# Attention blocks ordered by halves of the queries, with two buffers for the normalised block

## What is computed

```python
# layer 0: 16 heads of 32, rotary, biases, key mask
h = ada_norm(x, cond, ln1...)                   # norm, then scale and shift
q, k, v = heads(h @ wq + bq), heads(h @ wk + bk), heads(h @ wv + bv)
q, k = rotary(q), rotary(k)
attn = softmax(where(mask, q @ k.T / sqrt(32), -inf))
x = x + merge(attn @ v) @ wo + bo
x = x + gelu(ada_norm(x, cond, ln2...) @ ff_w1 + ff_b1) @ ff_w2 + ff_b2
# layer 1: 16 query heads on 4 key and value heads, no rotary
sh1, sc1, g1, sh2, sc2, g2 = split(silu(cond) @ wc.T + bc, 6)
x = x + g1 * (gqa(norm(x) * (1 + sc1) + sh1) @ wo.T)
x = x + g2 * (gelu((norm(x) * (1 + sc2) + sh2) @ w1.T + b1) @ w2.T + b2)
```

## Time and profile before

| what | us |
|---|---|
| median of 3 runs | 4369.27 (4364.93 to 4376.75) |
| the profiled execution, own time | 4378.7 |
| its span, from the first to the last instruction | 4376.9 |
| TensorE busy | 3913.1 |
| VectorE busy | 2427.8 |
| GpSimd busy | 1636.8 |
| ScalarE busy | 1618.2 |
| first score matmul starts | 136.80 |

### The profile page before, as it was taken

How to read it: one execution, slowest core, us unless ns; L and a number is a source line. 1 busy time by engine, 2 the same in 40 slices (tenths; PEclk the granted TensorE clock), 3 DMA queues, 4 the chain that set the end, 5 groups by cost and what they waited for, 6 DMA issues and landing times.

```text
span 4376.9 us, 53519 instructions
## 1 busy us (share of the span) xinstructions
PE 3913.1 (89%) x20400; PEld 1527.1 (35%) x20400; DVE 2427.8 (55%) x3944; ACT 1618.2 (37%) x2807; POOL 1636.8 (37%) x907
## 2 busy tenths in 40 slices
PE   6978899898998989989899998998899898989999
PEld 4312343233432234322243223432244223432234
DVE  3756635655455644556454666366554665556652
ACT  1456313553125531255411553135521553125521
POOL 2367212573115732156410563026510563115620
PEclk9889999989999999999999999999899999999999
DMA  4232242221422123232122021311122112310112
GB/s 133 59 90 107 69 106 73 68 62 56 102 74 64 54 78 91 76 80 67 67 87 87 15 65 57 105 37 42 37 87 92 28 35 71 100 57 18 62 55 95
DMA packets 140701, 307.44 MB, mean 70 GB/s; under 512 B 20336, under 2 KB 60292, under 8 KB 139552
## 3 DMA queue, kind: packets, MB, share of 16 engines
q10 hardware_dynamic: 50944, 174.62, 12.5%
q1 hardware_dynamic: 89504, 129.40, 11.3%
HBM read 225.56 MB, written 36.72 MB: 60 GB/s over the span
## 4 chain that ended last, share of the span: by engine, by line
PE 67%; DVE 13%; DMA 8%; POOL 5%; issue 4%; ACT 2%; SPq 1%; ACTq 0%; POOLq 0%; DVEq 0%
PE ps L774 11%; PE ps L775 11%; PE ps L776 11%; PE ps L954 8%; PE ps L875 7%; PE ps L937 6%; PE ps L811 6%; DMA dcopy<-inverses 5%; DVE mcol L1434 5%; PE ps L969 3%; POOL sums L691 3%; PE ps L828 2%; DMA inverses<-inverse 2%; ACT probs L1116 1%; DVE turn L1356 1%
## 5 line engine op out<-in xcount | busy, mean ns | idle before, releaser
L691 POOL TENSOR_TENSOR sums<-probs 128x1024 f32<-128x1024 f32 x480 | 1141.9, 2392 | 1513.4 <-ACT probs L1116 998.3
L1434 DVE TENSOR_REDUCE mcol<-ps 128x1 f32<-128x512 f32 x2048 | 1284.8, 684 | 543.1 <-PE ps L875 541.3
L1116 ACT ACTIVATE probs<-ps 128x512 f32<-128x512 f32 x2048 | 1105.0, 604 | 905.2 <-PE ps L937 614.4
L937 PE MATMUL ps<-qs,ks 98*128 98x512 f16 x2048 | 800.1, 402 | 190.0 <-ACT probs L1116 188.0
L875 PE MATMUL ps<-ks,qs 97*128 97x512 f16 x2048 | 809.7, 401 | 104.3 <-DVE mcol L1434 72.2
L954 PE MATMUL ps<-probs,v_sb 128*32 128x512 f32 x4096 | 597.2, 659 | 0.0
L1262 ACT ACTIVATE sums<-ps,cols 128x512 f32<-128x512 f32 x256 | 175.8, 687 | 1127.2 <-PE ps L776 1127.2
L875 PEld LDWEIGHTS ps<-ks,qs 97*128 97x128 f16 x2048 | 205.2, 100 | 723.3 <-DVE mcol L1434 385.9
L1520 DVE CAST probs<-sums 128x512 f16<-128x512 f32 x256 | 123.7, 483 | 501.8 <-ACT sums L1262 501.3
L774 PE MATMUL ps<-aT,ring 128*128 128x512 f16 x1024 | 392.2, 383 | 0.0
L775 PE MATMUL ps<-aT,ring 128*128 128x512 f16 x1024 | 391.2, 382 | 0.0
(11 more groups left out here) (106 smaller groups left out, 3221.9 us busy)
## 6 DMA issues: line engine op xcount, KB each, us to landing
ring<-halves ACTq DMA_DIRECT2D x208, 512.0 KB, 3.4
qs<-hl SPq DMA_DIRECT2D x192, 128.0 KB, 4.0
ring<-halves SPq DMA_DIRECT2D x48, 512.0 KB, 6.1
ring<-in_weights ACTq DMA_DIRECT2D x39, 512.0 KB, 4.4
halves<-ring ACTq DMA_DIRECT2D x37, 512.0 KB, 2.9
dcopy<-inverses SPq DMA_DIRECT2D x64, 256.0 KB
ks<-hl SPq DMA_DIRECT2D x120, 128.0 KB, 4.3
probs<-in_x SPq DMA_DIRECT2D x8, 1024.0 KB, 6.7
```

What stands on the lines that cost most here:

```text
L691: pool.tensor_tensor(sums[:, m % SUM_SLOTS, :, :], prob(u - 2), prob(u), ALU.add).then_inc(sum_set[0].sem, 1)
L937: pe.matmul(ps[:, bank, :], ks[0:K_EXP, key_set(i, hh), key_head(i, hh, h), P * kt:P * kt + P], qs[0:K_EXP, qc, h, :], start=True, stop=Tr ...
L1116: act.activation(prob(u)[:, e, :], ps[:, w % SCORE_BANKS, :], ACT.Exp).then_inc(exp_done.sem, 1)
L1434: dve.tensor_reduce(mcol[:, blk % 2, 4 * j + qt, half:half + 1], src, AX.X, ALU.max).then_inc(n_free[0], 1)
```

## The change

- `block_of` puts the halves of the queries outermost: blocks 0 to 3 are all heads of queries 0 to 511. The query stack `qs` is indexed by the half of the heads and overwritten by the second half of the queries at the steps 20 and 32. In layer 0 the second half of the keys is now used from block 2 on (before: block 4), so its projections, rotations and transfers move forward (`TURNS` in place of `ROTATE_AT`), and the maxima of block 2 start at step 8 (`MAX_AT_K`).
- `out_tile` waits for four finished blocks; its steps are 54 to 57 (n = 2 and 3 for the second half), `ln2` at 61 and 62, `norm_apply` of the second half at n = 4.
- `ocopy` has two buffers. `normalise` stands after addition 6 of the next block, ScalarE's `finish` at `w` = 11 of the block after that, GpSimd's after addition 1 there.
- Block 7 does not go through DRAM: VectorE inverts the whole `dcopy` (`invert_last`).
- `load_again` moves from `u` = 68 to 98, the bias additions of layer 0 to the additions 50 to 58, `deviation` of `ln2` from addition 56 to 55.
- At the start GpSimd's wait for the rows (`s_rows`) moves behind the first norms and builds.

```diff
--- before.py
+++ after.py
@@ -26,22 +26,23 @@
-O_AT, D_AT, HI_AT, INVERT_AT = 7, 12, 27, 4
+O_AT, D_AT, HI_AT, INVERT_AT, NORM_AT, LO_AT = 7, 12, 11, 4, 6, 1
...
-MAX_AT_0 = (0, 2, 5, 7, 9, 11, 14, 16, 18, 20, 23, 25, 27, 29, 32)
-WO_AT = 55
-LN2_AT = 62
-BIAS_AT = (40, 41, 42, 43, 48, 49, 54, 55)
-ROTATE_AT = ((1, 2, 6), (5, 6, 16), (14, 15, 31), (26, 28, 59))
+MAX_AT_K = (0, 2, 5, 7, 9, 11, 14, 16, 18, 20, 23, 25, 27, 29, 32)
+WO_AT = 54
+LN2_AT = 61
+BIAS_AT = (50, 51, 52, 53, 54, 55, 56, 58)
+TURNS = ((("k", 1, 0), -1, 1, 5), (("k", 1, 1), 3, 4, 11), (("q", 0, 1), 11, 13, 29), (("q", 1, 1), 25, 27, 57))
...
 def layer(i):
@@ -49,17 +50,18 @@
 def block_of(blk):
-    hh, r = divmod(blk, 4)
-    return hh, r // 2, r % 2
...
-def max_step(u):
+    qc, r = divmod(blk, 4)
+    return r // 2, qc, r % 2
...
+def max_step(i, u):
...
-        at = MAX_AT_0 if blk + 1 == 4 else MAX_AT
+        at = MAX_AT_K if layer(i) == 0 and blk == 1 else MAX_AT
...
-        items = [] if blk + 2 == 4 else [(blk + 2, k) for k in range(2 * (s - 14), 2 * (s - 13))]
+        items = [] if layer(i) == 0 and blk == 0 else [(blk + 2, k) for k in range(2 * (s - 14), 2 * (s - 13))]
@@ -85,12 +87,12 @@
-        for step, key in ((1, ("k", i, 1, 0, 0)), (2, ("k", i, 1, 0, 1)), (3, ("v", i, 1, 0)), (4, ("v", i, 1, 1)),
-                          (5, ("k", i, 1, 1, 0)), (6, ("k", i, 1, 1, 1)), (8, ("v", i, 1, 2)), (9, ("v", i, 1, 3))):
+        for step, key in ((0, ("k", i, 1, 0, 0)), (1, ("k", i, 1, 0, 1)), (2, ("v", i, 1, 0)), (3, ("k", i, 1, 1, 0)),
+                          (4, ("k", i, 1, 1, 1)), (6, ("v", i, 1, 1)), (7, ("v", i, 1, 2)), (9, ("v", i, 1, 3))):
...
-    for qc in range(2):
+    for hh in range(2):
...
-            at[11 + part if qc == 0 and layer(i) == 0 else 13 + 12 * qc + part] = [("q", i, 1, qc, part)]
+            at[11 + part if hh == 0 and layer(i) == 0 else 13 + 12 * hh + part] = [("q", i, hh, 1, part)]
@@ -119,8 +121,8 @@
-        if n in (3, 4):
-            keys += [("wo", i, 2 * n - 2), ("wo", i, 2 * n - 1)]
+        if n in (2, 3):
+            keys += [("wo", i, 2 * n), ("wo", i, 2 * n + 1)]
@@ -142,12 +144,13 @@
 def first_fills(j):
...
-        keys = [(kind, j, 0, th, part) for kind in "kq" for th in range(2) for part in range(2)]
+        keys = [("k", j, 0, th, part) for th in range(2) for part in range(2)]
+        keys += [("q", j, hh, 0, part) for hh in range(2) for part in range(2)]
...
-        keys += [("q", j, 0, th, part) for th in range(2) for part in range(2)]
+        keys += [("q", j, hh, 0, part) for hh in range(2) for part in range(2)]
@@ -277,7 +280,7 @@
-        ocopy = sb("ocopy", [P, D], F32)
+        ocopy = sb("ocopy", [P, 2, D], F32)
@@ -369,7 +372,8 @@
-        inv_part = count("inv_part", 8)
+        inv_part = count("inv_part", 7)
+        inv_last = count("inv_last", 1)
@@ -510,13 +514,13 @@
-                            dst = qs[r0:r0 + rows, th, heads, :]
+                            dst = qs[r0:r0 + rows, hh, heads, :]
...
             def put_rows(i, blk):
...
-                d = qs[97:98, qc, 4 * g:4 * g + 4, :]
+                d = qs[97:98, hh, 4 * g:4 * g + 4, :]
@@ -557,12 +561,12 @@
-                        if s == 9:
+                        if s == 7:
...
-                            put_stack(("q", i, 1, s // 32, part))
+                            put_stack(("q", i, s // 32, 1, part))
@@ -591,9 +595,6 @@
-                totals_out(i, 7)
-                inverse_in(i, 7)
-                if j < NB:
@@ -711,49 +712,57 @@
             def normalise(i, blk):
...
-                pool.wait_ge(inv_set.sem, inv_set.at(i, blk + 1))
-                pool.tensor_tensor(ocopy[:, :], ocopy[:, :], dcopy[:, :], ALU.mult).then_inc(a_set.sem, 1)
+                if blk < 7:
+                    pool.wait_ge(inv_set.sem, inv_set.at(i, blk + 1))
+                else:
+                    pool.wait_ge(inv_last.sem, inv_last.at(i, 1))
+                pool.tensor_tensor(ocopy[:, blk % 2, :], ocopy[:, blk % 2, :], dcopy[:, :], ALU.mult).then_inc(a_set.sem, 1)
...
             def finish(i, blk):
...
-                pool.tensor_tensor(aT[:, 1, 2 * hh + g, cut], ocopy[:, :], aT[:, 0, 2 * hh + g, cut], ALU.subtract
+                pool.tensor_tensor(aT[:, 1, 2 * hh + g, cut], ocopy[:, blk % 2, :], aT[:, 0, 2 * hh + g, cut], ALU.subtract
...
             def attention(i):
+                if layer(i) == 0:
+                    turns(i, -1)
...
-                    if m == 56:
-                        deviation("ln2", i, 0)
...
-                    if m >= 8 and m % 8 == 3:
+                    if m == 55:
+                        deviation("ln2", i, 0)
+                    if m >= 8 and m % 8 == NORM_AT:
...
-                    if m >= 8 and m % 8 == (4 if m // 8 == 6 else 5):
-                        finish(i, m // 8 - 1)
+                    if m >= 16 and m % 8 == LO_AT:
+                        finish(i, m // 8 - 2)
...
-                        for (turn_at, low_at, _), (kind, half) in zip(ROTATE_AT, (("k", 0), ("k", 1), ("q", 0), ("q", 1))):
-                            if m == turn_at:
-                                rotate((kind, i, 1, half, 0))
-                            if m == low_at:
-                                stack_low((kind, i, 1, half, 0))
+                        turns(i, m)
...
+            def turns(i, m):
+                for (kind, hh, th), turn_at, low_at, _ in TURNS:
+                    if m == turn_at:
+                        rotate((kind, i, hh, th, 0))
+                    if m == low_at:
+                        stack_low((kind, i, hh, th, 0))
...
             def first_builds(j):
...
-                    for kind in "kq":
-                        for th in range(2):
-                            rotate((kind, j, 0, th, 0))
-                            stack_low((kind, j, 0, th, 0))
+                    for key in (("k", j, 0, 0, 0), ("k", j, 0, 1, 0), ("q", j, 0, 0, 0), ("q", j, 1, 0, 0)):
+                        rotate(key)
+                        stack_low(key)
...
-            pool.wait_ge(s_rows, 64)
...
+            pool.wait_ge(s_rows, 64)
...
+                finish(i, 6)
@@ -832,8 +841,8 @@
             def out_tile(key):
...
-                pe.wait_ge(at_hi.sem, at_hi.at(i, 6 if tt < 4 else 8))
-                pe.wait_ge(at_lo.sem, at_lo.at(i, 6 if tt < 4 else 8))
+                pe.wait_ge(at_hi.sem, at_hi.at(i, 4 if tt < 4 else 8))
+                pe.wait_ge(at_lo.sem, at_lo.at(i, 4 if tt < 4 else 8))
@@ -935,7 +944,7 @@
-                          qs[0:K_EXP, qc, h, :], start=True, stop=True).then_inc(s_mm.sem, 1)
+                          qs[0:K_EXP, hh, h, :], start=True, stop=True).then_inc(s_mm.sem, 1)
...
             def values(i, u):
@@ -948,7 +957,7 @@
-                if u == 64 and layer(i) == 0:
+                if u == 32 and layer(i) == 0:
@@ -1095,11 +1104,11 @@
-                hi = act.activation(aT[:, 0, 2 * hh + g, 512 * qc:512 * qc + 512], ocopy[:, :], ACT.Identity, bias=bias_)
+                hi = act.activation(aT[:, 0, 2 * hh + g, 512 * qc:512 * qc + 512], ocopy[:, blk % 2, :], ACT.Identity, bias=bias_)
...
-                    hi = act.activation(ocopy[:, :], ocopy[:, :], ACT.Identity, bias=bias_)
+                    hi = act.activation(ocopy[:, blk % 2, :], ocopy[:, blk % 2, :], ACT.Identity, bias=bias_)
...
             def exps(i, w):
@@ -1117,9 +1126,9 @@
             def o_copy(i, blk):
...
-                if 8 * i + blk >= 1:
-                    act.wait_ge(at_lo.sem, at_lo.at(i, blk))
-                act.activation(ocopy[:, :], ps[:, 4, :], ACT.Copy).then_inc(o_out.sem, 1)
+                if 8 * i + blk >= 2:
+                    act.wait_ge(at_lo.sem, at_lo.at(i, blk - 1))
+                act.activation(ocopy[:, blk % 2, :], ps[:, 4, :], ACT.Copy).then_inc(o_out.sem, 1)
...
             def d_copy(i, blk):
@@ -1182,7 +1191,7 @@
             def load_again(i):
-                act.wait_ge(s_mm.sem, s_mm.at(i, 128))
+                act.wait_ge(s_mm.sem, s_mm.at(i, 192))
@@ -1210,8 +1219,8 @@
-                        if w % 32 == HI_AT:
-                            finish(i, blk - 1)
+                    if blk >= 2 and w % 32 == HI_AT:
+                        finish(i, blk - 2)
@@ -1223,9 +1232,9 @@
-                        for (_, _, hi_at), (kind, half) in zip(ROTATE_AT, (("k", 0), ("k", 1), ("q", 0), ("q", 1))):
+                        for (kind, hh, th), _, _, hi_at in TURNS:
...
-                                stack_high((kind, i, 1, half, 0))
+                                stack_high((kind, i, hh, th, 0))
@@ -1236,7 +1245,7 @@
-                    if u == 68:
+                    if u == 98:
@@ -1267,8 +1276,8 @@
-                    if n == 2:
-                        finish(i, 7)
+                    if n < 2:
+                        finish(i, 6 + n)
@@ -1328,7 +1337,7 @@
-                    dve.wait_ge(v_mul.sem, v_mul.at(i, STEPS // 2))
```

(9 more changed lines are left out.)

22 lines of the change are left out of this document (11 added, 11 removed).

## The result

| | us |
|---|---|
| before, median | 4368.16 (4364.93 to 4376.75, 4 runs) |
| changed, median | 4142.61 (4141.50 to 4144.66, 4 runs) |
| ratio | 0.9481, interval 0.9465 to 0.9498 |
| forecast | 4096 (4010 to 4235) |
| changed, the profiled execution: own time, span | 4144.66, 4142.9 |

The account below looks back on a forecast made before the run. The prediction took TensorE, busy 3913.1 of 4376.9 us, as the bound, with idle time and clock to win. Terms summed to 273 us off 4378.7, giving 4105.7; less 9.4 for the median, 4096 us, range 4010 to 4235.

Parts of the forecast that it names:

- Later places: Attention: moving `normalise` and `finish` later removes 150 of the score's 188.0 us wait for exponentials; bounds 80 and all.
- Output product: Attention: it waits for blocks 0 to 3 instead of a just finished block, gaining 30 us; bounds 25 and 33.
- Norm of the first half: End of attention: VectorE's norm one step earlier lets two chunks pass ahead of an addition, gaining 18 us; bounds 0 and 25.
- Clock: Attention: low clock behind removed stalls goes, half of 188 us not granted, 94 us; bounds 20 and 150.
- Rival 2: Attention: stalls go but short waits for banks hold the clock down, so 94 us don't come: 4190 us; chance 0.06.
- Forward part: Forward parts: earlier tiles and `norm_apply` put VectorE ahead by some us, gaining 25 of 40 us; bounds 0 and 40.
- Inversion in SBUF: Block 7: VectorE's reciprocal, taken as 4 us, delays `split` of the first chunk, losing 10 us; bounds 0 and 20.
- Keys earlier: Layer 0, step 8: a 2.7 us wait for the second key stack, four times with clock, loses 16 us; bounds 0 and 40.
- Other moves: Later second read of `x`, bias additions in block 6 and other new waits lose 25 us in all; bounds 0 and 60.
- Start: Kernel start: without GpSimd's wait for bias rows, VectorE's scales come earlier, gaining 7 us; bounds 3 and 8.
- the score's wait: Sign in the profile after: the score's wait for exponentials in attention comes near 40 us.
- the stacks: Sign in the profile after: a wait of 2 to 5 us for the stacks at step 8 in layer 0.

Follow-up runs that it names:

- experiment 6: Changed kernel with VectorE's addition 57 placed ahead of its normalisation of the first half: 4112.8 us, ratio 0.9399 to the kernel before.
- experiment 7: Kernel of experiment 6 with GpSimd's deviation behind addition 56 instead of 55: 4083.2 us, ratio 0.9357 to the kernel before.
- experiment 2: Changed kernel with only `normalise` put back behind addition 3: 4342.9 us, ratio 0.9919 to the kernel before.
- experiments 3 and 4: Changed kernel with all eight blocks inverted in SBUF, `normalise` behind addition 3 (4272.5 us) or behind addition 6 (4267.7 us).
- experiment 9: Changed kernel with block 7 inverted by way of DRAM again: 4178.9 us, ratio 0.9550 to the kernel before.
- experiment 8: Changed kernel with GpSimd's last bias additions ahead of the deviations in the forward part: 4097.7 us, ratio 0.9384 to the kernel before.
- experiment 4: Changed kernel with all eight blocks inverted in SBUF and `normalise` at its new place behind addition 6: 4267.7 us, ratio 0.9784 to the kernel before.
- experiment 11: Changed kernel with GpSimd waiting for the bias rows ahead of the first deviations again: 4150.6 us, ratio 0.9503 to the kernel before.

## Why the prediction was right, and where it was off

| term | forecast | measured |
|---|---|---|
| idle time in attention: 150 + 30 + 18 - 16 - 25 | 157 | 134.0 |
| clock in attention | 94 | 79.9 |
| forward parts: 25 - 10 | 15 | 14 |
| start | 7 | 7.5 |
| sum | 273 | 235 |

The measured terms of attention are from the two sums of windows; the forward parts, each from its last score to the next first one, add up to 1901.5 us before and 1887.3 after; the first score starts at 129.3 instead of 136.8. The windows are rounded, and the sum is 1 us over the 234.0 of the two executions.

*Later places: right, though the chain was read wrong in one link and stopped one link short.* 150 of the 188.0 us were to go. 111.9 went; with VectorE's addition mended (experiment 6) the wait is 35.2, so 152.8 of 188.0. The step that fell short is the one that put nothing on VectorE: the prediction listed what is queued behind `normalise` and `finish`, and for the norm of the first half it did not ask what is queued behind *that*. There, ScalarE's exponentials wait for VectorE's addition 57: 42.6 us, where it was 16.1 before. It booked this stall only as part of the unnamed 25 us of new waits; it cost 30 to 36 us by experiment 6 (medians and ratios), and more with experiment 7, which takes back what the swap costs in layer 0. The link read wrong is ScalarE: the prediction said that a wait for a transfer stops two engines that the scores need. GpSimd's stop alone costs 190 to 200 us (experiment 2), and ScalarE's stop in `finish` adds nothing to it.

*What made the old place bad* is settled by experiments 3 and 4: 190 to 200 us with the transfer, 5 without.

*Output product: right.* 30 forecast, and the wait of 32.8 us is gone whole. For the second half's tiles it took the inversion in SBUF as well: with block 7 by way of DRAM they wait 32.3 us at their new place (experiment 9).

*Norm of the first half: right in its own wait, given back next to it.* The wait of L792, now L801, for VectorE fell from 65.0 to 44.2. In the windows of the attentions, which the forecast was about, it fell from 22.8 to 7.2, by 15.6 where 18 were forecast; the other 5 us are in the forward parts. The addition behind it is what took that back.

*Clock: right.* The forecast half of what was not granted, 94 us; 79.9 came, with 85% of the idle time forecast. The mean of the attentions is 0.96, as forecast. Rival 2 held that short waits keep the clock down. The changed kernel still has them, 76.0 us in 130 pieces at L884 for `mcol` alone, but few of these lie in the attentions of layer 1 (6 pieces), whose clock is 0.97 and 0.98; 84 lie behind the last score of a batch. The stretch ahead of batch 1's attention holds 12 of those, of at most 0.6 us, at a clock of 1.00:

```profile
598.00:672.00 74.00, 65.30 (x295) 28.13 (x293) 36.07 (x62) 8.11 (x11) 0.25 (x1) 1.00 0.25 59
```

So waits as short as these do not hold the clock down. The rule of the Trainium skill, "TensorE: Matmul & The Clock Gate", section "A second HAM failure mode: psum-queue depth-cycling", that the cycling of banks makes the clock swing, did not decide here; for longer spells this row says nothing.

*Forward part: the sum right by luck, the mechanism wrong.* The prediction gave 25 of 40 us to VectorE being "ahead by some us". It is not ahead: seven waits of about 5 us are left of seven of 5.79, and the four operations still take 5.66 us beside GpSimd's eight additions. It named that neighbour and then let the lead, not the neighbour, decide; experiment 8 shows the neighbour did, and that 45 us lay there. Of the 14 us that came instead, some 11 are TensorE's busy time (1771.8 us before, 1760.7 after, at a mean clock of 0.98 and 0.98 to 0.99) and some 3 its idle time: the pieces for `hT` (8.2 us) and 5 us of the wait for `aT` went, and the wait of L978 for VectorE's addition grew from 5.8 us to 19.5.

*Inversion in SBUF: the price 3.35 us instead of 4, and no sign of its 10 us of loss.* The timeline of batch 5 shows it in its gap:

```profile
2996.66 0.60 ACT L1137 ACTIVATE dcopy<-ps 128x512 f32<-128x512 f32 x1 [2.90 <-PE ps L978]
...
2997.28 3.35 DVE L1460 RECIPROCAL dcopy<-dcopy 128x512 f32<-128x512 f32 x1 [1.90 <-ACT dcopy L1137]
...
3001.74 0.43 DVE L1534 CAST probs<-sums 128x512 f16<-128x512 f32 x1 [1.10 <-ACT sums L1271]
```

`split` waits 1.10 us for ScalarE after the reciprocal has ended, so here it delays nothing. And where the prediction set the route through DRAM at nothing, it would now cost 30 to 36 us (experiment 9), since the output product comes earlier. That the same reciprocal is dear where VectorE is on the path, experiment 4 shows: 56 of them in attention cost 125 to 132 us, 2.2 to 2.4 us each.

*Keys earlier: the wait is there, longer than forecast.* 20.6 us in four pieces, 5.0 to 5.6 each where 2.7 were worked out. The step is the 39 us at which SP was to reach `put_rows`: it did so at 712.33, 40 us into the attention, and the matmul that needs the keys could start 9.7 us later rather than 8.7; TensorE was there after 4.1 us (722.06 - 5.59 - 712.33), not 6. With its clock this is more than the 16 us.

*Other moves: less than forecast.* In the windows of the attentions the named waits of TensorE give 112 + 31 + 16 - 21 = 138 us, and its idle time fell by 134.0. So some 4 us of new waits lie outside them, not 25; but the stall behind VectorE's addition lies inside the first term.

*Start: right.* 7 forecast; the first score came 7.5 us earlier, and in experiment 11 it comes 7.8 us later again.

Of the signs named in the prediction these held: GpSimd's and ScalarE's waits, the clock, layer 1's attentions (238.0 to 241.7 us), the first score. These did not: the score's wait (76.1, not 40), the stacks (5.6, not up to 5), and in layer 0 a piece of 2.3 us is left at the end of block 2 in every batch, in the first one another at the end of block 5.

## What to carry to other kernels

An instruction that waits for a transfer belongs in an engine's queue where nothing urgent stands behind it: here three places later were worth 190 to 200 us, and without the transfer the two places were the same within the noise. When work moves, list what is queued behind it on its new engine too; the one addition that was missed cost 30 us or more. And look at which two engines work on the same memory side by side: moving two calls in GpSimd's queue, with no operation changed, gave 42 to 45 us.

## What the runs showed of the hardware that was not expected

- Some of VectorE's operations between SBUF tensors are held up by GpSimd's. Four operations 128x512 of L1343 take 1.91 us alone, 5.66 us (1.41 each) beside GpSimd's additions, which take 1.44 us each (11.52 for 8). At the end of attention, L1336 on 128x4 took 2.31 us and ended at 2969.00, where GpSimd's addition ended. The Trainium skill, "SBUF — State Buffer", section "SBUF: two separate sides", says that the two engines share a pair of ports, which a VectorE operation wants if it runs in a two-port mode or reads two SBUF tensors, and that whoever starts first holds it for the whole instruction. The trace agrees with the holding in these rows (one of VectorE's per addition of GpSimd's); the mode of L1343 is in no trace here. The maxima, read from PSUM, keep their 0.6 us beside GpSimd's additions (2.41 us for four in experiment 4), and the reciprocal there keeps its 3.34 although additions start on GpSimd 1.1 us after it.
- The reciprocal of 128x512 took 3.33 to 3.35 us in all 64 cases of each kernel of experiments 3 and 4, 6.5 ns an element of a partition. The estimate by the Trainium skill, "VectorE: DVE Perf Modes", section "First, the fixed hardware budget", was 4.3 us; the measurement decides.
- Waits of much the same length cost clock in one place and not in another. Behind the wait of 1.59 us in experiment 4 the first matmul took 0.39 us and the next of its kind 0.61, and the clock granted in the 5 us from 2943 on is 0.66. Behind the wait of 1.48 us in experiment 6 the matmul took 0.39, and the clock of the 7 us from 2943 on is 1.00. What TensorE had done before each was not separated.
